# One decoder layer on one core: the order in which attention weights are prepared, and where the logits stand

## The reference

```
x = x + GLA(LN(x))            # gated linear attention, 16 heads, key 16 wide, value 32 wide
    q, k*SCALE = x@Wq.T, x@Wk.T;  v = x@Wv.T;  gproj = x@Wg.T + bg
    gk = log_sigmoid(x@Wkg1.T@Wkg2.T + bkg2)/16
    S_t = S_{t-1}*exp(gk_t) + k_t v_t ;  o_t = q_t S_t
    o = (o - mean)/sqrt(var + eps) per head ;  out = (silu(gproj)*o) @ Wo.T
x = x + XATT(LN(x), ctx)      # 16 heads of 32; keys and values from ctx (112 rows) and, by other
                              # weights, from its last 16 rows ("dca"); q and k normed per head
x = x + MoE(LN(x))            # 4 experts, top 2 routing from logits, capacity 512 tokens each
```

## Time and profile before

| | value |
|---|---|
| median of three runs | 1053.38 us |
| the profiled execution's own time | 1052.63 us |
| its span | 1050.9 us |
| PE busy | 932.2 us, 89% |
| DVE busy | 697.7 us, 66% |
| POOL busy | 499.1 us, 47% |
| ACT busy | 453.1 us, 43% |
| share of PE in the chain that ended last | 74% |

### The profile page before, as it was taken

One profiled execution on the slowest core, in us unless ns is written; L12 is line 12 of the kernel. 1 busy time (PEld: TensorE's weight loads), 2 busy tenths in 40 slices (PEclk: granted clock), 3 DMA queues, 4 the chain that ended last, 5 costly groups with the idle time before them and its releaser, 6 DMA issues.

```text
span 1050.9 us, 19085 instructions
## 1 busy us (share of the span) xinstructions
PE 932.2 (89%) x7297; PEld 559.8 (53%) x7297; DVE 697.7 (66%) x1293; ACT 453.1 (43%) x754; POOL 499.1 (47%) x563
## 2 busy tenths in 40 slices
PE   3688999999999999999999663069999999999995
PEld 1446666766666766776676442034444444444342
DVE  6767677878887788778886545856554445345672
ACT  3444555565566655665555423122232333233210
POOL 1447677767677777767775720111070001003643
PEclk9788999999999999999999965569999999999998
DMA  8413000000000000000000006032335234335593
GB/s 289 133 51 128 4 15 18 5 17 17 15 2 17 17 14 14 6 17 14 17 2 14 11 12 229 26 115 83 118 90 191 80 121 160 100 100 198 159 243 121
DMA packets 40300, 78.39 MB, mean 75 GB/s; under 512 B 11378, under 2 KB 11650, under 8 KB 40258
## 3 DMA queue, kind: packets, MB, share of 16 engines
q1 hardware_dynamic: 35266, 63.13, 18.0%
q0 software_dynamic: 4992, 14.70, 5.1%
HBM read 64.16 MB, written 13.65 MB: 74 GB/s over the span
## 4 chain that ended last, share of the span: by engine, by line
PE 74%; DVE 7%; POOL 5%; issue 4%; DMA 4%; SPq 3%; ACT 1%; POOLq 0%; DVEq 0%; ACTq 0%
PE ps L1009 18%; PE ps L1010 17%; PE ps L1011 17%; PE ps L1015 6%; PE ps L1102 4%; PE ps L1181 3%; PE ps L1197 3%; POOL y_fetched L728 2%; PE ps L1206 2%; POOL hrs L596 2%; PE ps L1226 2%; DVE big L1674 1%; DMA y_fetched<-y_scratch,idx_get 1%; SPq L473 1%; PE ps L1114 1%
## 5 line engine op out<-in xcount | busy, mean ns | idle before, releaser
L596 POOL TENSOR_TENSOR hrs<-hve,neg_half 128x16 f32<-128x16 f32 x48 | 140.2, 2921 | 3.8
L982 ACT ACTIVATE big<-ps 128x512 f32<-128x512 f32 x64 | 38.2, 597 | 233.2 <-PE ps L1011 233.0
L1771 DVE TENSOR_SCALAR big<-big 128x512 f16<-128x512 f32 x64 | 27.8, 435 | 110.4 <-ACT big L982 110.3
L1009 PE MATMUL ps<-w2h,big 128*128 128x512 f16 x256 | 97.0, 379 | 2.5 <-DVE big L1363 2.5
L1009 PE MATMUL ps<-big,w1h 128*128 128x512 f16 x256 | 97.8, 382 | 1.4 <-DVE big L1363 1.4
L1011 PE MATMUL ps<-big,w1l 128*128 128x512 f16 x256 | 97.8, 382 | 0.0
L1010 PE MATMUL ps<-big,w1h 128*128 128x512 f16 x256 | 97.8, 382 | 0.0
L1010 PE MATMUL ps<-w2l,big 128*128 128x512 f16 x256 | 97.0, 379 | 0.0
L1011 PE MATMUL ps<-w2h,big 128*128 128x512 f16 x256 | 97.0, 379 | 0.0
L711 POOL DMA_INDIRECT big<-x_scratch,token_of x16 | 18.3, 1147 | 149.3 <-PE ps L1015 77.5
L728 POOL DMA_INDIRECT y_fetched<-y_scratch,idx_get x32 | 37.5, 1173 | 104.8 <-DMA y_scratch<-big 89.4
(11 more groups left out here) (305 smaller groups left out, 2530.5 us busy)
## 6 DMA issues: line engine op xcount, KB each, us to landing
wst<-in_w SPq DMA_DIRECT2D x28, 1024.0 KB, 5.2
x_scratch<-xn SPq DMA_DIRECT2D x16, 256.0 KB, 2.1
y_fetched<-in_w SPq DMA_DIRECT2D x4, 1024.0 KB, 13.4
out<-x_all SPq DMA_DIRECT2D x4, 1024.0 KB, 7.9
pr<-in_w_attn SPq DMA_DIRECT2D x3, 1024.0 KB, 8.4
x_all<-in_w_attn SPq DMA_DIRECT2D x3, 1024.0 KB, 11.7
x_all<-in_x SPq DMA_DIRECT2D x1, 3072.0 KB, 11.7
y_scratch<-big SPq DMA_DIRECT2D x3, 1024.0 KB, 6.1
```

Of the source, the lines that this page charges most:

```text
L596: pool.tensor_tensor(hrs[n][:, :], hve[n][:, :], neg_half[:, :], ALU.pow).then_inc(hdev[n], 1)
L982: act.activation(hg[f % 2], psum[f % 2][:, 512:1024], ACT.Gelu, scale=UN).then_inc(hg_r, 1)
L1009: nc.tensor.matmul(o, lh, rh, start=first, stop=False)
```

## The change

The pieces get another order: query-key is 0, values 1. Values are centred by Pool after DVE's means. The cross pieces' means, centring and splits are spread over steps 0 to 2. PE's first values product stands behind the first query-key product, and `second_kv` behind the values product of step 1. In every step the logits stand between two halves of the gate product, and on ACT `x3_out` stands ahead of xn2's `row_norm` and `logits_out` ahead of `x2_hi`.

```diff
-        pieces = [w_piece_of(c) for c in (C_V, C_QK, C_G, C_O)]
+        pieces = [w_piece_of(c) for c in (C_QK, C_V, C_G, C_O)]
-        POOL_CENTRED = (4, 5, 6)
+        POOL_CENTRED = (1, 4, 5, 6)
 SP
-            for n in range(3):
+            for n in (1, 0, 2):
                 weights(n)
 POOL
     deviation:  (n == 0)
+                if n == 0 and first(b, 0):
+                    centre(1)
                 if n == 0 and first(b, 1):
-                    centre(5)
-                    centre(6)
+                    centre(4)
     k_decay:
-                if first(b, 0):
-                    centre(4)
+                if first(b, 1):
+                    centre(6)
     gated:
+                if first(b, 0):
+                    centre(5)
 ACT
     split_hi:
-                if n == 0:
-                    act.wait_ge(cent, 2 * KC)
     x_hi:
+                if first(s[0], 1):
+                    gate_log_of(0)
     kg1_out:
-                if first(s[0], 0):
-                    split_hi(1)
                 if first(s[0], 1):
-                    split_hi(6)
+                    second_hi()
+                if first(s[0], 2):
+                    split_hi(7)
     log_sigmoid:
                 if first(b, 0):
-                    split_hi(2)
-                if first(b, 1):
-                    second_out()
-                    split_hi(7)
+                    split_hi(1)
     q_decay:
+                if first(s[0], 0):
+                    split_hi(2)
     k_decay:
                 if first(s[0], 0):
+                    v_out_of(0, 0)
                     split_hi(3)
+                if first(s[0], 1):
+                    second_out()
+                    split_hi(6)
     v_out, gate_log: skipped for sequence 0; gate_log no longer ends in second_hi()
     o_out:
-                if first(s[0], 0):
-                    split_hi(5)
     o_hi:
+                if first(s[0], 0):
+                    split_hi(5)
     body:
                 on(s[1], kv_out)
+                on(s[3], x3_out)
                 on(s[1], row_norm, 1, xn2, xn2_r)
                 on(s[0], ctx_hi)
-                on(s[3], x3_out)
+                on(s[3], logits_out)
                 on(s[1], x2_hi)
-                on(s[3], logits_out)
 PE
     a1_qk:
-                weights(b, 1)
+                weights(b, 0)
                 ...
+                if first(b, 0):
+                    weights(b, 1)
+                    rows(a1, xth, xtl, C_V, v_ps)
     a1_kg2:
-                if first(b, 1):
-                    second_kv()
     a1_v:
-                weights(b, 0)
-                rows(a1, xth, xtl, C_V, v_ps)
+                if not first(s[0], 0):
+                    rows(a1, xth, xtl, C_V, v_ps)
+                if first(s[0], 1):
+                    second_kv()
     body:
-                on(s[0], a1_g)
+                on(s[0], a1_g, range(KC // 2))
+                on(s[3], b2_logits)
+                on(s[0], a1_g, range(KC // 2, KC))
                 on(s[1], b1_x)
-                on(s[3], b2_logits)
 DVE
     a1_stats (sequence 0):   -centre_first()   +means(1)
     a1_weights:              -split_low(1) in step 0   +split_low(7) in step 2
     a1_sums (step 0):        -split_low(2), means(4)   +split_low(1)
     a1_decayed:              +split_low(2) in step 0, +split_low(6) in step 1
     a1_gate (sequence 0):    -means(5), means(6)
     a1_gate_log (seq. 0):    +means(5), second_low()
     a2_mask (sequence 0):    -second_low() behind the second, +means(4) behind the first
     a2_norm (sequence 0):    -split_low(6)   +means(6)
     a2_low (sequence 0):     +split_low(5) ahead of weights_cross, which loses split_low(7)
     b1_ctx (sequence 0):     -split_low(5)
```

More of the change, by code:

```diff
@@ L824, in k_decay, with v_out_of, gate_log_of @@
                 if first(s[0], 0):
+                    v_out_of(0, 0)
                     split_hi(3)
+                if first(s[0], 1):
+                    second_out()
+                    split_hi(6)
+            def v_out_of(b, par):
+                after(act, v_ps, b)
+                take(v[par][:, :], a1, UN, v_r)
             def v_out(s):
                 b, par, half = s
-                after(act, v_ps, b)
-                take(v[par][:, :], a1, UN, v_r)
+                if not first(b, 0):
+                    v_out_of(b, par)
             def gate_log(s):
                 b, par, half = s
+                if not first(b, 0):
+                    gate_log_of(b)
+            def gate_log_of(b):
                 after(act, gf_r, b)
@@ L1016, in turn, with rows @@
                 last.then_inc(done, 1)
-            def rows(ps, xh, xl, col, done, opens=True):
-                for k in range(KC):
+            def rows(ps, xh, xl, col, done, opens=True, ks=range(KC)):
+                for k in ks:
                     last = mm3(ps, xh[:, k, :], xl[:, k, :], wh[:, k, col:col + D], wl[:, k, col:col + D], opens and k == 0, k == KC - 1)
-                last.then_inc(done, 1)
+                if k == KC - 1:
+                    last.then_inc(done, 1)
             def second_kv():
@@ L1075, in a1_kg2, with a1_v, a1_g @@
                 last.then_inc(kg2_ps, 1)
[L1076 removed]
+            def a1_v(s):
+                if not first(s[0], 0):
+                    rows(a1, xth, xtl, C_V, v_ps)
+                if first(s[0], 1):
                     second_kv()
[L1079 to L1084 removed]
+            def a1_g(s, ks):
                 b, par, half = s
@@ L1087, in a1_g @@
                 after(pe, v_r, b)
-                rows(a1, xth, xtl, C_G, g_ps)
+                rows(a1, xth, xtl, C_G, g_ps, ks=ks)
             def a2_scores(s, rnd):
@@ L1448, in a1_stats @@
                 if first(b, 0):
-                    centre_first()
+                    means(1)
             def a1_low(s):
@@ L1457, in a1_weights @@
             def a1_weights(s):
-                if first(s[0], 0):
-                    split_low(1)
+                if first(s[0], 2):
+                    split_low(7)
             def a1_sums(s):
@@ L1472, in a1_sums @@
                 if first(b, 0):
-                    split_low(2)
-                    means(4)
+                    split_low(1)
             def a1_decayed(s):
@@ L1483, in a1_decayed @@
                                              ALU.mult, ALU.mult)
+                if first(b, 0):
+                    split_low(2)
                 after(dve, dke_r, b)
@@ L1492, in a1_decayed @@
                     split_low(3)
+                if first(b, 1):
+                    split_low(6)
             def a1_gate(s):
@@ L1496, in a1_gate @@
                 dve.scalar_tensor_tensor(gf[:, :], a1, UN, bg_sb[:, :], ALU.mult, ALU.add).then_inc(gf_r, 1)
-                if first(s[0], 0):
-                    means(5)
-                    means(6)
             def a1_gate_log(s):
@@ L1503, in a1_gate_log @@
                 dve.scalar_tensor_tensor(ge[:, :], gf[:, :], 0.0, ge[:, :], ALU.min, ALU.subtract).then_inc(gl_r, 1)
+                if first(s[0], 0):
+                    means(5)
+                    second_low()
             def a2_mask(s, rnd):
@@ L1509, in a2_mask @@
                 dve.copy_predicated(groups(scm[:, rnd * 1024:(rnd + 1) * 1024]), mask, groups(psum[1][:, :])).then_inc(scm_r, 1)
-                if rnd and first(s[0], 0):
-                    second_low()
+                if not rnd and first(s[0], 0):
+                    means(4)
             def a2_norm(s):
@@ L1515, in a2_norm @@
                 if first(s[0], 0):
-                    split_low(6)
+                    means(6)
             def a2_low(s):
@@ L1537, in b1_ctx @@
                 low(ctl[:, :, :], ctx32[par][:, :, :], XS, cth[:, :, :]).then_inc(ctl_r, 1)
-                if first(b, 0):
-                    split_low(5)
             def b1_k_norm(s):
```

14 lines of the change are left out of this document (4 added, 10 removed).

## The result

| | before | after |
|---|---|---|
| median of five runs | 1053.38 us (1051.51 to 1055.26) | 1059.92 us (1057.40 to 1060.63) |
| the profiled execution's own time | 1052.63 us | 1057.89 us |
| its span | 1050.9 us | 1056.0 us |
| PE, DVE, POOL, ACT busy | 932.2, 697.7, 499.1, 453.1 us | 933.0, 694.9, 504.8, 450.1 us |

The ratio is 1.0064, interval 1.0046 to 1.0081: slower by 6.5 us, where 1054.0 was forecast with a range to 1058.3. The forecast missed on the slow side.

What follows compares the result with a forecast made beforehand. TensorE's own queue was taken to bound the kernel from the fourth step on. On 1052.63 us, -3.5 +1.7 +3.3 +0.5 -1.0 = +1.0 gives 1053.6, as median 1054.4; forecast 1054.0, range 1048.8 to 1058.3.

Steps and rivals of the forecast that it cites:

- start -3.5: Up to the first turn of xn2: the new weight order gains 3.5 us (bounds 1.3 to 6.4).
- step 2 +1.7: Piece 7's splits ahead of q's copy and softmax, plus half clock, give back 1.7 us (0.5 to 3).
- full steps: Logits between gate halves: later xn2 turn delays the masked product, net 0.30 us a step, 3.3 lost over 11 steps.
- clock: Half-clock stretches in turn, logits, scores: moving logits out gains 1.0 us (bounds 3.3 gained, 1.7 lost).
- drain: Last steps: x3T's copy, now first on ScalarE, and the logits delay xn2's turn by 0.5 us.
- S: Time in step 1 when ScalarE is through with dca's high parts: 45.1 us, or 42.5 with everything at full clock.
- B: Rival, slower: the masked product waits in each full step, net 0.45 us; +4.5 in all, 1058; chance 0.23.
- A: Rival: late xn2 turn is absorbed, mask meets its reader, each step gains 0.1 us; -3.5, 1049.5; chance 0.22.
- C: Rival: the start gives its bound, 5 us, with the wait in the steps; -2.2, 1051; chance 0.1.

Runs made afterwards that it cites:

- e10: Kernel of e1 plus 28 dummy matmuls in the wait ahead of the first turn of xn2: 1056.47 us, ratio 1.0000 to before.
- e1: Kernel after with the end of each step in before's order, so only the weight order is new: 1055.98 us, ratio 1.0022 to before.
- e4: Both kernels with dummy matmuls in the drain's waits: after 1046.93 us, ratio 0.9933; before 1044.00 us, ratio 0.9919, each to the unfilled before.
- e3: Kernel after with before's order of logits and xn2's turn in steps 16 to 18 only: 1055.95 us, ratio 1.0013 to before.
- e5: Kernel after with six dummy matmuls behind xn2's turn in step 16 only: 1056.28 us, ratio 1.0017 to before.
- e2: Kernel before with only the logits moved between the gate halves and ScalarE's copies with them: 1056.39 us, ratio 1.0026 to before.
- e6: Kernel before with logits, then xn2's turn, between the gate halves in full steps; weights and drain unchanged: 1050.96 us, ratio 0.9979 to before.
- e8: Kernel before with logits and xn2's turn between gate product parts in full steps, plus dummy matmuls in steps 1, 2 and drain: 1040.53 us, ratio 0.9855.
- e0: Kernel after run once more unchanged, for a second look at its clock: 1059.30 us, one run.

## Why the prediction was wrong

Put together by stretch, in us, with the pooled profiles of above:

| stretch | forecast | the profiled pair | pooled |
|---|---|---|---|
| start to step 3 (start -3.5, step 2 +1.7) | -1.8 | +0.6 | +2.1 |
| full steps with their clock (+3.3, -1.0) | +2.3 | -0.6 | 0 |
| drain | +0.5 | +5.7 | +4.3 |

The remaining -0.6 of the pair lies in the routing and the experts. By the pooled profiles two parts failed by nearly 4 us each: the drain, by its clock, and the start, of which step 2 alone is 2.3. The full steps were forecast 2 us too slow, and by luck that took back a part.

- **Clock, -1.0, and drain, +0.5: the step that failed.** The prediction looked for the clock where before's profile showed short dips, at 150 and 563, and counted the logits' move as a gain there. Both dips are gone in the profile after, as expected. Over the profiles that is borne out for the full steps: none of the six with the new end has a dip there; of the four with the old one before has one and e10 two, and e1 and e4 before have none. What decides is the drain, for which the clock term has no line. With the logits first, PE does 1.06 us of 4-column matmuls, a turn of 0.6 and two waits, 0.74 and 1.42, and then runs q's product at half clock and the output products largely so: 4.3 us as a mean over nine profiles. e3, e4 and e5 show it from three sides. As an order the drain was rightly called cheap: at a kept clock (e4) nothing is lost there. The price was put on the delay of the turn and not on what the delay does to the clock. The bound of the clock term, a loss of 1.7, took a dip's 1.6 us as the largest step, while the clock line of before, 6, 5, 5 and 6 tenths from 604 us on, said that more was at stake.
- **Step 2, +1.7: the second.** Right in sign, but half the size: +3.4 in the pair, +4.0 pooled. The prediction names the place, piece 7's low part ahead of the softmax, and prices both splits at 1.3 at the turn of the gated output and 0.9 behind it. That turn comes 26.81 us after xn2's instead of 23.19: 2.04 more between the two score rounds, 0.46 more ahead of the first (PE waits for ACT's `qT`, behind the high part), and 1.2 from the clock, priced at 0.8. The 6 us of idle ahead of xn2's turn was foreseen (6.75), and PE then runs at half clock up to 84.2, which before did from 78.2 to 85.2 as well. The clock can be won back there with dummies (3.5 us, e1 against e10), but most of what the new order adds is the splits.
- **Start, -3.5.** The first mask ended at 35.10 (34.5 was forecast) and the turn of xn2 at 74.80 (73.7 to 74): -2.8, and -1.9 pooled, within its bounds. The chain behind S held link by link and was 1 us late: the low part of piece 5 took 2.95 us instead of 2.3 beside Pool's centring. Pool's centrings took 6.12 and 6.56 us, slower than 4.06, beside DVE's low parts. Piece 6's high part ended at 66.97 (the forecast's S+22.4 is 67.0, with S at 44.6), 1.67 us ahead of its low part at 68.64, so it cost nothing. The exclusion that the Trainium skill, "SBUF — State Buffer" (SBUF: two separate sides), gives for two-input VectorE operations and reading GpSimd operations agrees: four centring operations take 2.1 and 2.5 us more with a low part of 2.3 and 2.95 beside them, and two of piece 5 without one take 2.05, half of 4.06.
- **Full steps, +3.3.** The mechanism held link by link: power 6.92 behind the scores (6.9 forecast), masked product later by 0.37 (0.39 forecast). The size was off because the logits' place saves 0.25 us and not 0.1 (turn of x3 to the scores: 4.62 before, 4.37 after). Net 0.12 a step instead of 0.30, 1.1 us from step 3 to step 16 where the clock holds in both, which the absence of a dip of 1.6 hides in this pair.
- **Rivals.** B had the sign and, at 1058, nearly the size, by luck: its place, the masked product, costs a net 0.12 us a step, not 0.45. A is dead (34.30, not 34.1), and C too (2.8 at the first turn, all given back by step 3; not 5).

What stays open: why the clock falls in one order and holds in the other is not shown, only that it does. e2 measured +2.7 us (1.2 to 4.3), where the pooled drain and its period make 4.2 to 5.4; whether this is chance isn't settled. Why e6 gains with a longer period isn't either.

## What to carry to other kernels

Price a moved TensorE instruction twice: by who waits for it, and by the waits that it leaves bare. Here waits of 0.74 and 1.42 us ahead of a dependent chain of large matmuls came with a clock loss of 4.3 us, several times the added idle time. Price a preparation that is moved into a later step by what stands behind it there: one low part of 2.28 us ahead of a softmax delayed TensorE by 2.04. Treat written-out first and last steps as kernels of their own, since an order that is right in a full step can be wrong where its neighbours are missing. Where a wait can't be removed, matmuls into a free PSUM bank in front of the chain are cheap to try, and comparing two orders with such fillers in both tells order from clock, if the granted clock of the compared windows is the same.

## What was not expected of the hardware

- Useless work gained time: 8.1 thousandths for the kernel before by the drain's fillers alone (e4), 14.5 with steps 1 and 2 and the better step order (e8). One filler matmul takes 0.22 to 0.24 us (28 in 6.21, 6 in 1.46).
- The clock can fall with TensorE busy all the time. In the profile of before, the stretch ahead of the dip at 149.8:

```profile
143.00:149.80 6.80, 6.71 (x63) 4.77 (x62) 4.44 (x15) 4.01 (x9) 4.20 (x6) 1.00 0.19 58
```

6.71 of 6.80 us busy, then 0.50. The Trainium skill, "TensorE: Matmul & The Clock Gate" (HAM oscillation — how this bites in real kernels), warns of idle gaps of TensorE; here there is next to none. The gate product of twelve 512-column matmuls ends at 146.8, and what follows is short: a turn, 4-column logits and 64-column scores. A busy TensorE did not keep the clock here; what did make it fall is not shown.
- A part of the half-clock stretches differs between executions of one kernel (after has one of 3.4 us at 582.5, e0 one of 6.9 us at 579.7 in its place). The single runs of before reach from 1049.1 to 1060.6 us over all passes.
